# Attention: one power of 16 columns in place of two of 8 on GpSimd, scatters and fetched results at other units, bias matmuls on 128 rows

## The reference, cut to what matters

```python
q, k, v = x @ Wq.T + bq, x @ Wk.T + bk, x @ Wv.T + bv      # 16 heads; q and k two maps of 8 each
q1, q2, k1, k2 = rope(...)
a1, a2 = softmax(causal(q1 @ k1.T * scale)), softmax(causal(q2 @ k2.T * scale))
out = (a1 - lam * a2) @ v
out = out * rsqrt(mean(out * out, -1) + 1e-6)              # for each head
out = (out * head_norm_w * (1 - LAMBDA_INIT)) @ Wo.T + bo
```

## Time and profile before

| | |
|---|---|
| median of 3 runs | 1314.96 us (1312.19 to 1315.63) |
| the profiled execution | 1313.84 us, its span 1312.1 us |
| busy over the span | PE 83%, DVE 75%, POOL 65%, ACT 55% |
| granted TensorE clock | 0.94 over the span, 1.00 in the turns between 564 and 635 us |
| a routes turn, 564.25 to 599.75 us | 35.50 us: PE 33.05 busy, DVE 30.83, POOL 27.50, ACT 23.89 |
| a places turn, 599.75 to 634.75 us | 35.00 us: PE 32.57 busy, DVE 31.30, POOL 28.54, ACT 24.86 |

### The profile page before, as it was taken

How to read it: one execution, slowest core, us unless ns; L and a number is a source line. 1 busy time by engine, 2 the same in 40 slices (tenths; PEclk the granted TensorE clock), 3 DMA queues, 4 the chain that set the end, 5 groups by cost and what they waited for, 6 DMA issues and landing times. The chain is left out here.

```text
span 1312.1 us, 33095 instructions
## 1 busy us (share of the span) xinstructions
PE 1086.2 (83%) x11868; PEld 783.7 (60%) x11868; DVE 982.9 (75%) x2544; ACT 723.3 (55%) x1311; POOL 854.0 (65%) x1032
## 2 busy tenths in 40 slices
PE   2653996489999999999999998569994897999697
PEld 1432775256666666666666665358884574666466
DVE  6882885588888898989898876368885965788672
ACT  4721654446667666766667676245663654444173
POOL 4873777225667787878788777653775324889651
PEclk9985999899999999999999999679997798999999
DMA  8113431110000011101111010043323100000001
GB/s 260 44 50 104 113 107 53 28 41 24 20 24 22 24 35 32 34 22 36 32 33 36 24 28 8 17 141 96 105 86 114 49 1 1 1 0 1 1 25 41
DMA packets 63982, 62.80 MB, mean 48 GB/s; under 512 B 11088, under 2 KB 53488, under 8 KB 63440
## 3 DMA queue, kind: packets, MB, share of 16 engines
q1 hardware_dynamic: 54384, 39.66, 11.5%
q0 software_dynamic: 9440, 21.02, 4.7%
HBM read 28.10 MB, written 24.17 MB: 40 GB/s over the span
## 5 line engine op out<-in xcount | busy, mean ns | idle before, releaser
L1847 ACT ACTIVATE diff_prob<-diff_st_ps 128x512 f32<-128x512 f32 x384 | 227.8, 600 | 159.7 <-PE diff_st_ps L2290 154.6
L1996 DVE TENSOR_REDUCE diff_q_pack<-diff_s_ps 128x2 f16<-128x512 f32 (+1 forms) x384 | 262.2, 692 | 63.0 <-PE diff_s_ps L2273 60.7
L1782 POOL TENSOR_SCALAR_AFFINE_SELECT diff_prob<-diff_prob 128x256 f32<-128x256 f32 (+1 forms) x384 | 188.4, 499 | 121.8 <-ACT diff_prob L1847 119.1
L431 POOL DMA_INDIRECT exp_ys<-moe_y_sb,moe_dest x156 | 153.1, 982 | 87.7 <-ACT moe_y_sb L514 45.9
L2273 PE MATMUL diff_s_ps<-diff_k_one,diff_qT 128*128 128x128 f16 (+1 forms) x1024 | 147.9, 247 | 0.0
L2290 PE MATMUL diff_st_ps<-diff_qmT,diff_k_one 128*128 128x256 f16 (+1 forms) x1024 | 147.1, 247 | 0.3 <-ACT diff_prob L1847 0.2
L2313 PE MATMUL diff_ot_ps<-diff_prob,diff_v 128*32 128x128 f32 x3072 | 125.4, 282 | 9.8 <-POOL diff_prob L1782 7.6
L507 ACT ACTIVATE moe_h_hi<-moe_h 128x512 f16<-128x512 f32 x94 | 59.2, 630 | 88.4 <-DVE moe_h L737 88.4
L1749 POOL TENSOR_TENSOR diff_rms<-diff_ms,all_neghalf 128x8 f32<-128x8 f32 x64 | 105.1, 1643 | 3.6 <-DVE diff_ms L2020 2.8
L2273 PEld LDWEIGHTS diff_s_ps<-diff_k_one,diff_qT 128*128 128x128 f16 x1024 | 89.7, 98 | 22.1 <-issue 0.4
L2313 PEld LDWEIGHTS diff_ot_ps<-diff_prob,diff_v 128*32 128x32 f32 x3072 | 73.3, 110 | 45.2 <-issue 23.6
(11 more groups left out here) (397 smaller groups left out, 2988.5 us busy)
## 6 DMA issues: line engine op xcount, KB each, us to landing
moe_xg<-exp_xs SPq DMA_DIRECT2D x78, 130.0 KB
diff_k_one<-diff_kT SPq DMA_DIRECT2D x128, 64.0 KB, 2.0
diff_yg<-exp_ys SPq DMA_DIRECT2D x14, 256.0 KB, 2.9
fetched_yg<-exp_ys SPq DMA_DIRECT2D x7, 512.0 KB, 4.0
exp_ys<-moe_y_sb,moe_dest POOLq DMA_INDIRECT x156, 2.3
all_x<-in_x SPq DMA_DIRECT2D x4, 512.0 KB, 5.1
moe_up<-in_w SPq DMA_DIRECT2D x16, 128.0 KB, 3.8
out<-all_x SPq DMA_DIRECT2D x8, 256.0 KB, 2.3
```

Source lines behind the costliest of these rows:

```text
L431: nc.gpsimd.indirect_dma_start(out=ew.ys, out_offset=bass.IndirectOffsetOnAxis(ap=dest[:, s, j:j + 1], axis=0), in_=y_sb[:, s % YR, j], in ...
L1782: nc.gpsimd.affine_select(out=pr, in_=pr, compare_op=ALU.is_ge, fill=0.0, base=0, pattern=[[0, n], [1, P]], channel_multiplier=-1).then_in ...
L1847: nc.scalar.activation(prob[:, u % RING], st_ps[:, u % 2], ACT.Exp, scale=SCALE).then_inc(exp_ready, 1)
L1996: nc.vector.tensor_reduce(q_pack[:, par, j, m0:m0 + n, 3 * HD], s_ps[:, u % 2].rearrange("p (m k) -> p m k", m=n), op=ALU.max, axis=AX.X, ...
```

## The change

The power is taken once per half, of 16 columns in two blocks of 8. All scatters of the turns with four of them go to units 16, 18, 20 and 22. They were at 10, 13, 16, 18 in places turns and at 5, 16, 18, 20 in routes turns. The turn with eight keeps its units. Fetched results are added in units 1 and 3 where A is even (routes turns) and in units 15 and 17 where A is odd (places turns). They were added in units 5 and 9 of every turn. SP issues the fetch after the first half of `k_one` instead of after the second. ACT's copy `exp_xT` and DVE's taking of the ranks go from unit 4 to unit 3. The bias operands get 128 rows. Rows 64 and up of `two_ones` are zero.

```diff
-    SEND_AT = {0: (10, 13, 16, 18, 19, 20, 22, 23), 4: (5, 16, 18, 20)}
+    ADD_AT = ((1, 3), (15, 17))
+    SEND_AT = {4: (16, 18, 20, 22), 8: (10, 13, 16, 18, 19, 20, 22, 23)}
...
-        bias_rows = nm.sb("bias_rows", [2 * LO, QKV], F16)
-        two_ones = nm.sb("two_ones", [2 * LO, P], F16)
-        wo_rows = nm.sb("wo_rows", [2 * LO, P], F16)
+        bias_rows = nm.sb("bias_rows", [P, QKV], F16)
+        two_ones = nm.sb("two_ones", [P, P], F16)
+        wo_rows = nm.sb("wo_rows", [P, P], F16)
...
                         sp.dma_start(k_one[rows, par, r, ch], kT[rows, ch]).then_inc(k_one_ready[half], 16)
-                if ew and A + 2 < NB:
-                    if A >= 1:
-                        sp.wait_ge(fetch_added, A * 4)
-                    sp.dma_start(yg[:], ew.results[:, 2 * A + 4:2 * A + 6]).then_inc(fetched, 16)
+                    if ew and half == 0 and A + 2 < NB:
+                        if A >= 1:
+                            sp.wait_ge(fetch_added, A * 4)
+                        sp.dma_start(yg[:], ew.results[:, 2 * A + 4:2 * A + 6]).then_inc(fetched, 16)
...
-            def rms_of(b, half, j):
-                if j == 0:
-                    pool.wait_ge(ms_ready, b * 2 + half + 1)
+            def rms_of(b, half):
+                pool.wait_ge(ms_ready, b * 2 + half + 1)
                 heads = slice(8 * half, 8 * half + 8)
-                nc.gpsimd.tensor_tensor(rms[:, j, heads], ms[:, j, heads], neghalf[:, 0:8], ALU.pow).then_inc(rms_ready, 1)
+                nc.gpsimd.tensor_tensor(rms[:, :, heads], ms[:, :, heads], neghalf[:, 0:16].rearrange("p (j h) -> p j h", j=2),
+                                        ALU.pow).then_inc(rms_ready, 1)
...
-                    if sends and u in SEND_AT[sends[1]] and sends[1] + SEND_AT[sends[1]].index(u) < sends[2]:
-                        scatter(sends[0], sends[1] + SEND_AT[sends[1]].index(u))
+                    if sends and u in SEND_AT[sends[2] - sends[1]]:
+                        scatter(sends[0], sends[1] + SEND_AT[sends[2] - sends[1]].index(u))
...
-                    if D is not None and u in (1, 2):
-                        rms_of(D, 0, u - 1)
-                    if D is not None and u in (7, 8):
-                        rms_of(D, 1, u - 7)
+                    if D is not None and u == 1:
+                        rms_of(D, 0)
+                    if D is not None and u == 7:
+                        rms_of(D, 1)
...
-                    g = routes if u == 4 and places is None else norms if u == 21 and norms == routed - 1 else None
+                    g = routes if u == 3 and places is None else norms if u == 21 and norms == routed - 1 else None
...
-                once(nc.vector.tensor_copy(bias_rows[:], qkv_bias[0:2 * LO]))
+                once(nc.vector.tensor_copy(bias_rows[:], qkv_bias[:]))
...
-                once(nc.vector.tensor_copy(wo_rows[:], wo_bias[0:2 * LO]))
+                once(nc.vector.tensor_copy(wo_rows[:], wo_bias[:]))
...
-                if u == 4:
+                if u == 3:
                     take_ranks(g)
...
-                            dve.wait_ge(rms_ready, D * 4 + 4)
+                            dve.wait_ge(rms_ready, D * 2 + 2)
...
-                        if u in (5, 9) and 1 <= A < NB - 1:
-                            add_fetched(A, (u - 5) // 4)
+                        if u in ADD_AT[A % 2] and 1 <= A < NB - 1:
+                            add_fetched(A, ADD_AT[A % 2].index(u))
```

## The result

| | before | after |
|---|---|---|
| median (4 runs each) | 1314.72 us | 1290.55 us (1288.69 to 1294.33) |
| ratio, 95% interval | | 0.9817, 0.9804 to 0.9831: 24 us faster |
| profiled execution | 1313.84 us | 1294.33 us, its span 1292.6 |
| granted clock over the span | 0.94 | 0.932 |
| C = 0 begins, C = 15 begins | 289.90, 806.57 us | 293.43, 789.79 us |

A forecast was written before the change was run, and what follows sets the result against it. Neither PE nor DVE alone was taken to bound the kernel; the lead passes between them. Gains per turn, last turns and bias summed to 11.5 us: 1313.84 to 1302.3 profiled, 1303.5 forecast as median, range 1293 to 1314.

The forecast's parts named there:

- `on`, held again: Routes turn: POOL's addition still holds `on`, which ends at 580.6 to 580.9 instead of 581.78, 0.9 to 1.2 us earlier.
- an unheld `on`: Lower bound of the forecast: if POOL no longer holds `on`, 0.8 x 9 = 7 us less.
- my own case: The forecast's main outcome for the whole kernel: 1296 to 1310 us, chance 0.49.
- the projections lie in the stretch that DVE leads: Projections, units 6 to 13: the bias saving there is covered; last turns and fill keep about 0.3 us.
- The price for each change of rows: PE matmuls: each change between 64 and 128 rows costs 0.09 to 0.10 us; twelve per turn, 1.15 us.
- My first rival: PE leads everywhere, so the bias counts in full, up to 16 us: 1288 to 1295 us, chance 0.12.
- Routes turn: Turns with even A: 1.1 us shorter each, five turns giving 5.5 us; PE gains 0.3 us before L2425.
- Places turn: Turns with odd A: `on` 1.0 us earlier, less 0.8 for new adds; net 0.2 us, four turns giving 0.8.
- The price that I set on the new adds: Places turns, units 15 and 17: adds delay `weighted` and L2497 by 0.3 to 2.0 us, taken as 0.8.
- The power: POOL, each half: 16 columns take 2.90 us, 0.39 less per half, without holding up DVE.
- The scatters: Routes turn: with unit 5's scatter gone, POOL can start the power near 575.3 instead of 575.89.
- The last turns: C = 14 gains 1.3 us, C = 15 0.8, its tail 0.4; C = 13 0.6, C = 0 to 3 1.8.

The follow-up runs named there:

- late_on: Kernel after with a 0.27 us DVE memset ahead of `on` in unit 9; ratio to before 0.9892, stage 503.45 us.
- bias_adds: Kernel before with only the 128-row bias and the moved adds with early fetch; ratio to before 0.9938, stage 509.08 us.
- no_bias: Kernel after with the bias operands on 64 rows again; ratio to before 0.9897, stage 505.51 us.
- no_scatter: Kernel after with the scatters in their old units again; ratio to before 0.9918, stage 508.16 us.
- no_power: Kernel after with two powers of 8 columns per half again; ratio to before 0.9831, stage 498.45 us.
- twins: Kernel after with POOL's addition in unit 10, bias on 64 or 128 rows; ratios to before 0.9889 and 0.9829, stages 504.95 and 495.92 us.
- only_bias: Kernel before with only the bias operands on 128 rows; ratio to before 1.0011, stage 520.51 us.
- rot_10: Kernel before with POOL's first rotation addition in unit 10 instead of 9; ratio to before 0.9963, stage 514.58 us.
- add_16_19: Kernel after with the adds of odd-A turns in units 16 and 19; ratio to before 0.9823, stage 499.93 us.
- on_11: Kernel before with `on` taken in unit 11 instead of 10; ratio to before 0.9970, stage 514.12 us.
- add_13_17: Kernel after with the adds of odd-A turns in units 13 and 17; ratio to before 0.9893, stage 509.47 us.

## Why the prediction was right in direction and short by half

- **What failed first: "`on`, held again".** I laid out `on` at 579.1 and POOL's addition at 579.0, that is 14.85 and 14.75 us into the turn, and called the race lost by 0.1 us. In the trace they stand at 14.33 and 14.36: won by 0.03. A layout that is half a microsecond off cannot call a race of 0.1. I should have kept both outcomes as cases. Nor was the hold itself read rightly: I took it as that of the addition alone, and wrote that for L1804 the trace agrees with the rule of one instruction. In the routes turn of before, `on` (to 581.78) also waited through the mask behind the addition, which ends at 581.50. The 7 us that I gave an unheld `on` as a bound is close to what late_on lost by holding it again, 7.08; I had it in my own case's range, but not together with the next point. The mask:

```profile
581.10 0.40 POOL L1782 TENSOR_SCALAR_AFFINE_SELECT diff_prob<-diff_prob 128x256 f32<-128x256 f32 x1
```

- **What failed most: "the projections lie in the stretch that DVE leads".** True before, false after: with its add gone and `on` free, DVE idles in unit 11, and PE leads. I sized the bias at 0.3 us; it is worth 9.03 with the race settled. The price for each change of rows was right, about 0.10 us, but the projections have six that cost something, 0.63 us a turn, and not eight. Right was the cover of the other four changes of the twelve: the two output matmuls save PE a further 0.34 us by the second L2470 (22.56 before, 20.12 after, 2.44 us less), and L2486 keeps 2.10 of it, as it waits for `k_pack`.
- **The cover was undone by the change itself.** I judged each edit against the kernel before. But the edits that relieve DVE decide whether one that relieves PE counts. bias_adds shows it directly: 7.59 us together, none apart. My first rival, that the bias counts in full, had 0.12 and the time that came, 1288 to 1295. That it named the time is in part luck. Its 16 us were too many: two of the twelve changes cost nothing and four stay covered, which leaves six, or 9 us in 15 turns; the rest of the gain comes from `on`, unit 5 and the scatters.
- **Routes turn: 1.1 forecast, 2.10 measured.** By undoing, L2452 owes 0.62 to the bias, 0.57 to the adds, 0.54 to unit 3 and 0.29 to the scatters: 2.02, near the 2.10. (The turns of no_bias and no_scatter show 0.78 and 0.45, with the 0.16 us at L2425 that are chance.) L2425 gained 0.55 instead of 0.3, because `xT_lo` ended 6.21 us into the turn and not 6.85. The wait didn't change its owner; it went.
- **Places turn: 0.2 forecast, 1.18 measured.** 1.75 us at L2452 instead of 1.0; and from there to unit 19 it gives 0.56 back instead of 0.8. The price that I set on the new adds was about right. The first pair stands beside L1795 and takes 1.02 us, the second 0.75.
- **The power: right.** 2.92 us on the average of 32, 2.90 forecast, and it holds none of DVE's adds: two ran in 0.60 us inside it (564.56). no_power gives it 2.1 us of the stage. The rule of the Trainium skill's page "SBUF — State Buffer", section "SBUF: two separate sides", would have let it block them for its whole length; for the power the trace does not agree.

```profile
L1749 POOL TENSOR_TENSOR diff_rms<-diff_ms,all_neghalf 128x16 f32<-128x16 f32 x32 | 93.5, 2922 | 3.8 <-DVE diff_ms L2021 3.8
```

- **The scatters: wrong.** I took their move as a detail of POOL's start, and it is worth 11.8 us by undoing it. They set when POOL comes to its mask and its addition, hence which of the two engines is first and how many instructions `on` waits through.
- **The last turns.** C = 14 gained 1.92 us (1.3 forecast), C = 13 1.37 (0.6), C = 0 to 3 together 2.42 (1.8). Too small throughout. Undoing the scatters costs C = 14 1.88 us and undoing the power 0.70; undoing unit 3 costs C = 13 1.06 and undoing the bias 0.67. With C = 15, `on` comes 1.05 us earlier (12.61 instead of 13.66 us into the turn, and 13.65 in no_power: that is the power), and from the begin of C = 15 to the last `on` the kernel after takes 37.78 us instead of 40.73: 2.95 gained, 1.2 forecast.
- **By terms.** The four undoings without the power cost 9.1, 14.0, 8.1 and 11.8 us, 43 in all for a gain of 20.3. Three of them bring back meetings of DVE and POOL in some turns that cost more than the edit's own work: the adds and unit 3 in places turns, the scatters in routes turns. The bias does not, as its twins show. The costs overlap, so the 20.3 can't be shared out among the edits.

**What stays open.** Why the near tie falls as it does: `on` started 0.18 us ahead of the addition both in the kernel after (0.50 us) and in only_bias (3.02), each time beside a mask that had about 0.2 us to go. Why rot_10 leaves `on` held in routes turns alone. One thing is common to the 16 cases in these runs in which `on` waited beyond the addition, or through several masks: POOL had a pause of 0.04 to 2.4 us right behind the last of them. Where it waited for the addition alone, the next mask stood directly behind, and `on` went ahead of it. The runs don't show why POOL goes first in the one case and DVE in the other. And why add_16_19 costs the places turn 0.63 us.

## What to carry to other kernels

Before an edit is costed at nothing because another engine leads, ask what the other edits do to that engine: relieve the leader first, then cost the rest against what leads next. Where a short DVE instruction starts within 0.1 to 0.3 us of a long POOL one, take both outcomes as cases with their own chances, and rather than rely on the order, try one of the two a unit away, and see in the trace whether it is free: on_11 freed `on` everywhere, rot_10 did not. Count what POOL has to do directly behind such a meeting: where it ran several instructions back to back, the hold lasted up to four of them. And compare more than one turn of each kind, with its granted clock, before an effect of 0.15 us a turn is read from one.

## What was not expected of the hardware

- A DVE instruction with two SBUF inputs is not always held for one POOL instruction only. `on`, 0.41 us when free, took 1.26 us beside the addition alone, 1.82 beside the addition and a mask, and 2.62 and 3.02 us beside more. In each of the held cases it ended 0.28 us after the end of the POOL instruction that held it last: in late_on the addition ends at 624.89 and `on` at 625.17, in only_bias the third mask ends at 636.67 and `on` at 636.95. How many it waits through differs. In no_bias the mask behind the addition let it go first. In only_bias three masks did not. The Trainium skill's page "SBUF — State Buffer", section "SBUF: two separate sides", speaks of the whole length of the one instruction that started first; the longest POOL instruction beside the 3.02 us took 1.25.
- POOL gives way as well: the addition took 1.50 us behind an `on` that started 0.03 us ahead of it, and 1.25 to 1.27 where `on` waited for it.
- A power of 2.92 us on POOL holds none of DVE's adds, which have two SBUF inputs: in the kernel after, 12 adds ran inside one, each in 0.335 to 0.344 us, the shortest of all adds. An addition of 1.25 us does hold them.
- A change between matmuls of 64 and 128 rows costs PE about 0.10 us each way inside a projection (0.31 us for three), and nothing in front of the projection, behind a matmul of 128 rows and 32 columns or an idle time. The Trainium skill's page "TensorEngine Tiling (Array Packing)", section "Key Properties", says that the array drains at such a change, and gives no price.
- The granted clock can fall to its lower level in the middle of the stage. In add_13_17, PE stands idle for 2.28 us before L2486 in five turns (0.81 in the kernel after). In each of the five, the clock went from 1.00 to 0.50 for 3.41 us, at the earliest 0.4 us before L2486 and at the latest 1.4 us behind its start, and the way from L2486 to L2497 took 7.1 to 7.4 us instead of 6.0. It also fell once each in only_bias and no_scatter, near L2452, where PE had idled 1.94 and 1.03 us in unit 12, and not in the other turns of these runs that look the same.
